# Middle stage: x^T by 256-byte loads and VectorE's 32x32 transposes, q, k and v as three fp32r products, mask in two instructions

## The reference

```python
Q, K, V = (X @ Wq.T, X @ Wk.T, X @ Wv.T)          # 16 heads of 16
KV  = einsum('blhd,blhe->blhde', K, V)
Y   = einsum('blhd,blhde->blhe', Q, cumsum(KV, axis=1))
Bm  = Lm @ swapaxes(Lm, -2, -1)                    # Lm = Ltri * tril
Y   = einsum('hed,blhd->blhe', Bm, Y).reshape(...)
out = Y @ Wc.T
x = x + 0.5 * ffn(layernorm(x)); x = x + attn(layernorm(x)); x = x + 0.5 * ffn(layernorm(x))
```

## Time and profile before

| | us |
|---|---|
| median of three runs (2888.28 to 2891.92) | 2888.59 |
| the profiled execution's own time | 2889.19 |
| its span, first to last instruction | 2887.4 |
| TensorE busy (95%) | 2743.9 |
| TensorE weight loads busy (86%) | 2480.5 |
| VectorE busy (59%) | 1702.5 |
| ScalarE busy (45%) | 1311.9 |
| GpSimd busy (42%) | 1202.6 |

### The profile page before, as it was taken

One profiled execution on the slowest core, in us unless ns is written; L12 is line 12 of the kernel. 1 busy time (PEld: TensorE's weight loads), 2 busy tenths in 40 slices (PEclk: granted clock), 3 DMA queues, 4 the chain that ended last, 5 costly groups with the idle time before them and its releaser, 6 DMA issues.

```text
span 2887.4 us, 56040 instructions
## 1 busy us (share of the span) xinstructions
PE 2743.9 (95%) x18295; PEld 2480.5 (86%) x18295; DVE 1702.5 (59%) x4037; ACT 1311.9 (45%) x2765; POOL 1202.6 (42%) x1550
## 2 busy tenths in 40 slices
PE   4499999999999999989999995999999999999999
PEld 3389899999999989878888884898999998999988
DVE  8754555465555555457878875445555454555554
ACT  5644444454444444334444443444444444444443
POOL 3744444545454545310111122454445454454543
PEclk8699999999999999999999997999999999999999
DMA  8644345353434343221111013434344434434332
GB/s 246 202 99 93 62 92 103 57 100 60 99 61 97 64 92 63 47 62 35 56 62 59 32 46 98 99 58 89 72 97 80 79 60 94 100 58 101 62 53 41
DMA packets 320886, 233.07 MB, mean 81 GB/s; under 512 B 181296, under 2 KB 292784, under 8 KB 320688
## 3 DMA queue, kind: packets, MB, share of 16 engines
q0 software_dynamic: 62688, 87.11, 18.7%
q1 hardware_dynamic: 247712, 133.06, 18.1%
q10 hardware_dynamic: 10288, 10.38, 1.1%
HBM read 124.32 MB, written 78.79 MB: 70 GB/s over the span
## 4 chain that ended last, share of the span: by engine, by line
PE 52%; DVE 3%; issue 1%; ACT 0%; DVEq 0%; POOL 0%; DMA 0%; ACTq 0%; POOLq 0%
PE e_ps L106 8%; PE e_ps L107 8%; PE e_ps L108 8%; PE e_psy L1248 5%; PE mi_qk L1534 3%; PE e_psx L1248 3%; PE e_psy L1250 3%; PE mi_sc L1550 2%; PE mi_yo L1570 2%; PE e_psx L1250 2%; PE mi_yo L1597 2%; PE mi_xv L1540 2%; DVE mi_prob L1715 1%; PE mi_kv L1584 1%; PE mi_yo L1561 1%
## 5 line engine op out<-in xcount | busy, mean ns | idle before, releaser
L1367 DVE TENSOR_TENSOR e_hid<-e_ps,e_gate 128x384 f32<-128x384 f32 (+1 forms) x640 | 382.5, 598 | 394.0 <-ACT e_gate L1306 392.7
L1375 DVE TENSOR_TENSOR e_h_lo<-e_hid,e_h_hi 128x384 fp32r<-128x384 f32 (+1 forms) x640 | 385.0, 602 | 257.3 <-ACT e_h_hi L1310 257.3
L1306 ACT ACTIVATE e_gate<-e_ps 128x384 f32<-128x384 f32 (+1 forms) x640 | 335.4, 524 | 441.1 <-PE e_ps L108 427.7
L1310 ACT ACTIVATE e_h_hi<-e_hid 128x384 fp32r<-128x384 f32 (+1 forms) x640 | 357.2, 558 | 360.8 <-DVE e_hid L1367 348.8
L106 PE MATMUL e_ps<-e_xT_hi,c_wa 128*128 128x384 f32 (+1 forms) x1280 | 448.9, 351 | 5.6 <-issue 5.3
L107 PE MATMUL e_ps<-e_xT_lo,e_wb 128*128 128x384 f32 (+1 forms) x1280 | 450.6, 352 | 0.0
L106 PE MATMUL e_ps<-e_xT_hi,e_wb 128*128 128x384 f32 (+1 forms) x1280 | 450.5, 352 | 0.0
L108 PE MATMUL e_ps<-e_xT_hi,e_wb 128*128 128x384 f32 (+1 forms) x1280 | 450.5, 352 | 0.0
L107 PE MATMUL e_ps<-e_xT_lo,c_wa 128*128 128x384 f32 (+1 forms) x1280 | 448.4, 350 | 0.0
L108 PE MATMUL e_ps<-e_xT_hi,c_wa 128*128 128x384 f32 (+1 forms) x1280 | 448.2, 350 | 0.0
L467 POOL DMA_INDIRECT c_xrow<-normed_rows,e_token x320 | 352.4, 1101 | 153.3 <-POOL e_token L1133 77.9
(11 more groups left out here) (305 smaller groups left out, 4755.3 us busy)
## 6 DMA issues: line engine op xcount, KB each, us to landing
c_raw<-w SPq DMA_DIRECT2D x544, 64.0 KB, 2.6
e_spread<-c_xrow SPq DMA_DIRECT2D x608, 32.0 KB
c_raw<-w SPq DMA_DIRECT2D x68, 256.0 KB, 4.1
e_spread<-c_xrow SPq DMA_DIRECT2D x640, 24.0 KB
normed_rows<-r_xn SPq DMA_DIRECT2D x8, 1056.0 KB, 7.1
normed_rows<-mi_xn SPq DMA_DIRECT2D x8, 1056.0 KB, 4.9
x<-x ACTq DMA_DIRECT2D x8, 1024.0 KB, 12.3
out<-mi_x SPq DMA_DIRECT2D x8, 1024.0 KB, 5.3
```

Source lines behind the costliest of these rows:

```text
L1306: act.activation(gate[:, f % 2, 0:n], ps1[f % 2][:, 0:n], ACT.Silu).then_inc(gated, 1)
L1310: act.activation(h[0][:, f, 0:n], hid[:, f % 2, 0:n], ACT.Copy).then_inc(h_high, 1)
L1367: dve.tensor_tensor(hid[:, f % 2, 0:n], ps3[f % 2][:, 0:n], gate[:, f % 2, 0:n], ALU.mult).then_inc(hid_ready, 1)
L1375: dve.tensor_tensor(h[1][:, f, 0:n], hid[:, f % 2, 0:n], h[0][:, f, 0:n].bitcast(F32), ALU.subtract).then_inc(h_ready, 1)
```

## The change

In the middle stage, chunks go in pairs for x^T, q and k. x^T of a pair no longer comes from TensorE: SyncE loads x1 again from DRAM in blocks of 32 rows by 64 columns (four DMAs a pair, 256 bytes a piece), VectorE transposes their 32x32 squares in one instruction (`square`), ScalarE rounds the result to fp32r (`high_x`), GpSimd subtracts (`low_x`). q and k of the pair and v of each chunk become three fp32r products each. q of a pair is made in the odd steps and k in the even ones, in one bank after the other; ScalarE's copies of q and k have 512 columns in place of 256. k's turn goes to v's bank and waits until v is kept. The mask is two instructions of 1024 columns. The rows of the weights are permuted by the host to fit the order in which squares come out. The steps begin at -6. GpSimd's picked rows are now tied to steps 4 and 5. In the routing stage ScalarE and VectorE split the centred weights into a high and a low part; some of Setup's tiles now lie in the expert stage's row tile, so `keep_heads` also waits for the low part.

```diff
@@ class Setup
+    def split_high(self, act):
+        k = self.k
+        act.wait_ge(self.centered, 1)
+        act.activation(k.wqk[0][:], self.raw_qk[:], ACT.Copy)
+        act.activation(k.wvr[0][:], self.raw_vr, ACT.Copy).then_inc(self.heads_ready, 1)
+
+    def split_low(self, dve):
+        k = self.k
+        dve.wait_ge(self.heads_ready, 1)
+        dve.tensor_tensor(k.wqk[1][:], self.raw_qk[:], k.wqk[0][:].bitcast(F32), ALU.subtract)
+        dve.tensor_tensor(k.wvr[1][:], self.raw_vr, k.wvr[0][:].bitcast(F32), ALU.subtract).then_inc(self.centered, 1)
...
     def keep_heads(self, act):
-        act.wait_ge(self.heads_made, 1)
+        act.wait_ge(self.heads_made, 2)
+        act.wait_ge(self.centered, 2)
...
@@ route_phase, ScalarE: for each group g, behind the normalisation of group g+1
+                    if g == 0:
+                        su.split_high(act)
                     if g == 1:
                         su.keep_heads(act)
@@ route_phase, VectorE: at the end of group g
                     if g == 0:
                         su.center(dve)
+                    if g == 1:
+                        su.split_low(dve)
@@ middle_phase, SyncE
+                for n in STEPS:
+                    if pair_at(n + 6) is not None:
+                        spread_rows(pair_at(n + 6))
+                    if n == -6:
+                        load(1)
+                        load(2)
...
@@ middle_phase, GpSimd
+                def low_x(p):
+                    pool.wait_ge(x_high, p + 1)
+                    pool.tensor_tensor(xT[p % 2][1][:], turned[:], xT[p % 2][0][:].bitcast(F32),
+                                       ALU.subtract).then_inc(x_low, 1)
+
+                for n in STEPS:
+                    g, c = divmod(n, MG)
+                    if pair_at(n + 4) is not None:
+                        low_x(pair_at(n + 4))
+                    if c in (4, 5) and 1 <= g < MGS:
+                        r.pick_rows(pool, g - 1, (g - 1) % 2, MQ * (g - 1) + c - 4, c - 4)
@@ middle_phase, TensorE
+                def project_q(p):
+                    pe.wait_ge(x_low, p + 1)
+                    wait(pe, qk_kept, 2 * p)
+                    for blk in range(KD):
                         for kk in range(KD):
+                            ins = mm3(pe, qk[:, blk * 2 * P:(blk + 1) * 2 * P], wqk(kk, blk),
+                                      (xT[p % 2][0][:, kk, :], xT[p % 2][1][:, kk, :]), kk == 0, kk == KD - 1)
                     ins.then_inc(qk_made, 1)
...
                 def turn_k(n):
-                    pe.wait_ge(q_kept, n + 1)
+                    pe.wait_ge(qk_kept, n // 2 * 2 + 2)
+                    pe.wait_ge(v_kept, n + 1)
...
                 for n in STEPS:
                     g, c = divmod(n, MG)
-                    if chunk(n + 2):
-                        project_qk(n + 2)
+                    if pair_at(n + 3) is not None:
+                        project_q(pair_at(n + 3))
+                    if pair_at(n + 2) is not None:
+                        project_k(pair_at(n + 2))
+                    wait(pe, kr_kept, min(n + 2, NCH))
...
@@ middle_phase, ScalarE, step n
+                    if pair_at(n + 3) is not None:
+                        keep_q(pair_at(n + 3))
+                    if pair_at(n + 2) is not None:
+                        keep_k(pair_at(n + 2))
                     if chunk(n + 2):
...
+                        keep_v(n + 2)
                     if chunk(n):
                         keep_y(n)
                     if chunk(n + 2):
                         keep_krow(n + 2)
-                    if chunk(n + 3):
-                        keep_x(n + 3)
+                    if pair_at(n + 4) is not None:
+                        high_x(pair_at(n + 4))
@@ middle_phase, VectorE
-                    for i in range(4):
-                        dve.tensor_tensor(prob[n % 2][:, i], sc[:, i, :].rearrange("p (h t) -> p h t", h=4),
-                                          k.causal[:].unsqueeze(1).broadcast_to([P, 4, P]),
+                    for i in range(0, 4, 2):
+                        dve.tensor_tensor(prob[n % 2][:, i:i + 2].rearrange("p i h t -> p (i h) t"),
+                                          sc[:, i:i + 2, :].rearrange("p i (h t) -> p (i h) t", h=4),
+                                          k.causal[:].unsqueeze(1).broadcast_to([P, 8, P]),
...
+                    if pair_at(n + 5) is not None and n > -2:
+                        square(pair_at(n + 5))
```

More of the change, by code:

```diff
@@ L1464, in middle_phase, with pair_at, own @@
         xn2_stored = [m.sem(f"xn2_stored{b}") for b in range(2)]
-        vzero = m.sem("vzero")
         tab_kept = m.sem("tab_kept")
         x1_g, x2_g, xn_g = (groups_of(t) for t in (x1_in, x2_out, xn_out))
-        STEPS = range(-2, NCH + TAB + 1)
+        STEPS = range(-6, NCH + TAB + 1)
+        PAIRS = NCH // 2
+        SPREADS = 16 * QUARTERS
+        def pair_at(n):
+            return n // 2 if n % 2 == 0 and chunk(n) else None
+        def own(n):
+            return slice(n % 2 * P, n % 2 * P + P)
         def chunk(n):
@@ L1491, in load, with spread_rows @@
                     sp.dma_start(x1[:, g % 3], x1_g[g]).then_inc(x_loaded[g % 3], 16)
-                load(1)
-                load(2)
-                for g in range(MGS):
-                    sp.wait_ge(x2_ready, MG * (g + 1))
-                    sp.dma_start(x2_g[g], x2[:, g % 2]).then_inc(x2_stored[g % 2], 16)
-                    if g + 3 < MGS:
-                        load(g + 3)
-                    sp.wait_ge(xn2_made, MG * (g + 1))
-                    sp.wait_ge(r.gated, g + 1)
-                    sp.dma_start(xn_g[g], xn2[:, g % 2]).then_inc(xn2_stored[g % 2], 16)
+                def spread_rows(p):
+                    wait(sp, x_squared, p)
+                    for j in range(QUARTERS):
+                        rows = x1_in[p * 2 * P:(p + 1) * 2 * P, j * KD * SQ:(j + 1) * KD * SQ]
+                        sp.dma_start(spread[j * SQ:(j + 1) * SQ, :, :],
+                                     rows.rearrange("(u s) d -> s u d", s=SQ)).then_inc(x_spread, 16)
+                for n in STEPS:
[5 more added lines that the diff above has]
+                    g, c = divmod(n, MG)
+                    if c == 0 and 1 <= g < MGS + 1:
+                        sp.wait_ge(x2_ready, MG * g)
+                        sp.dma_start(x2_g[g - 1], x2[:, (g - 1) % 2]).then_inc(x2_stored[(g - 1) % 2], 16)
+                        if g + 2 < MGS:
+                            load(g + 2)
+                    if c == 4 and 1 <= g < MGS + 1:
+                        sp.wait_ge(xn2_made, MG * g)
+                        sp.wait_ge(r.gated, g)
+                        sp.dma_start(xn_g[g - 1], xn2[:, (g - 1) % 2]).then_inc(xn2_stored[(g - 1) % 2], 16)
                 for b in range(2):
@@ L1520, in _, with wqk @@
             def _(pe):
-                def turn_x(n):
-                    wait_x1(pe, *divmod(n, MG))
-                    wait(pe, v_kept, n)
-                    for half in range(KD):
-                        ins = pe.transpose(xv[:, half * P:(half + 1) * P],
-                                           x1[:, n // MG % 3, n % MG, half * P:(half + 1) * P], k.ident[:])
-                    ins.then_inc(xt_made, 1)
-                def project_qk(n):
-                    pe.wait_ge(xT_ready, n + 1)
-                    wait(pe, kr_kept, n)
-                    for blk in range(2 * KD):
-                        for kk in range(KD):
-                            ins = pe.matmul(qk[:, blk * P:(blk + 1) * P], k.wqk[:, kk, blk * P:(blk + 1) * P],
-                                            xT[n % 2][:, kk, :], start=(kk == 0), stop=(kk == KD - 1))
+                def wqk(kk, blk):
+                    return tuple(part[:, kk, blk * P:(blk + 1) * P] for part in k.wqk)
@@ L1536, in project_qk @@
                     ins.then_inc(qk_made, 1)
                 def project_v(n):
+                    high, low = xT[n // 2 % 2]
                     for kk in range(KD):
-                        ins = pe.matmul(xv[:, 0:WV], xT[n % 2][:, kk, :], k.wvr[:, kk, :],
-                                        start=(kk == 0), stop=(kk == KD - 1))
+                        ins = mm3(pe, xv[:, 0:WV], (high[:, kk, own(n)], low[:, kk, own(n)]), (k.wvr[0][:, kk, :], k.wvr[1][:, kk, :]),
+                                  kk == 0, kk == KD - 1)
@@ L1549, in scores @@
                             rows = slice(32 * i, 32 * i + 32)
-                            ins = pe.matmul(sc[:, i, half * 2 * P:(half + 1) * 2 * P], kT[n % 2][rows, half, :],
-                                            qeo[n % 2][rows, half].rearrange("p a t -> p (a t)"),
+                            ins = pe.matmul(sc[:, i, half * 2 * P:(half + 1) * 2 * P], kT[n // 2 % 2][rows, half, own(n)],
+                                            qeo[n // 2 % 2][rows, n % 2, half].rearrange("p a t -> p (a t)"),
```

(13 more changed lines are left out.)

121 lines of the change are left out of this document (59 added, 62 removed).

## The result

The changed kernel takes 2917.22 us (median of four runs, 2913.34 to 2919.08) by 2890.26 for the kernel before (2888.28 to 2893.54): 1.0094 of it, interval 1.0082 to 1.0106, slower. The forecast was 2911, with a range of 2892 to 2930. The profiled execution took 2913.34 us, its span 2911.4, at a granted clock of 0.975; the sum of the prediction, 2911.6, is made against this kind of number. It is the fastest of the four, though: by medians the change costs 27.0 us, in the two profiled executions 24.0, and the sum said 22.4.

The account below looks back on a forecast made before the run. The prediction took TensorE to bound the middle stage and ScalarE's queue to set the routing stage's end. It summed 2889.2 + 12.2 routing + 10 start + 3.0 six full groups - 2.8 last group = 2911.6, given as 2911, range 2892 to 2930.

Parts of the forecast that it names:

- Routing, +12.2: Routing stage: keep_heads on ScalarE waits for VectorE's split_low, so group 3's normalisation comes later; +12.2 us, between 8 and 13.
- the routing hides its wait: Routing stage: the wait disappears in the slow issue of copies, +1 in place of +12, 2899 us; chance 0.08.
- Start, +10: Start of the middle stage: loads, square, high and low parts precede the first q; chunk 0 10 us later, bounds 6 and 14.
- Hand-over: Middle stage, odd steps: q waits 1.65 us for GpSimd's subtraction; two steps take 14.35 us, where they took 14.36.
- the walk: Middle stage: eight steps timed by TensorE's output and VectorE's addition; 59.6 us with rounding, +0.5 for each of six groups.
- VectorE: Middle stage: mask -0.13 us a step, transposition 0.62 to 0.70 in odd steps; work 53.5 a group, 52.1 before, below 59.
- the ranks' wait: Middle stage, step 3: VectorE reads the ranks 1.0 us later, since ScalarE keeps q of two chunks before v.
- The last chunks, -2.8: Middle stage, last group, which ends without q, k and turn of k: -2.8 us.
- The rival on the other side: Middle stage: the hand-over's 1.65 us is hidden, full groups take 57.0; 2886 us, no change; chance 0.12.
- The clock rival: Middle stage: each 1.65 us idle drops TensorE to half clock, some 1.5 us a pair, +48, 2959 us; chance 0.05.

Follow-up runs that it names:

- low_early: The changed kernel with VectorE making the weights' low part before reading group 1's ranks, in place of after that group's picks: 2910.93 us, 1.0066 of the kernel before.
- low_twice: The changed kernel with GpSimd's subtraction done twice for each pair, the first into a tile nobody reads: 2985.98 us, 1.0328 of the kernel before.
- high_early: The changed kernel with ScalarE's high_x behind the keeping of v, in place of behind the copy of k's rows: 2913.66 us, 1.0085 of the kernel before.
- moments_together: stats_seven with VectorE's moments of x1 for the next group interleaved with x2's in step 0, from the second group on: 2888.85 us, 0.9999 of the kernel before.
- stats_seven: The changed kernel with low part and high_x earlier, squares behind the addition, start loads reordered, x1 statistics in steps 6 and 7: 2888.99 us, 1.0006 of the kernel before.

## Why the prediction was right

The two large terms and both mechanisms behind them were right: ScalarE's wait for the low part in the routing stage, and GpSimd's pass on the path of each pair. That the sum comes within 2 us of the profiled execution is in part luck. The terms missed by -2.1, -0.2, +0.8, +3.1 and -0.3, which cancel in part, and by medians the change costs 27.0 where the sum said 22.4.

- **Routing, +12.2, measured +10.1.** The wait for the low part ended at 76.74 (76.2 forecast). Behind it, the work up to the next normalisation took 9.6 us, not 11.1: the two copies (the forecast once says three) are now issued in 1.37 us in place of 2.22, and ScalarE no longer waits between its own two copies of the head products, 0.4 us. Of the 11.4 by which that normalisation is late, 10.1 reach the end of the expert stage. The bounds (8 to 13) held it. low_early takes 7.8 of it back at that mark by removing this wait alone, so the rival "the routing hides its wait" is out.
- **Start, +10, measured +9.8.** Less the 10.1 us by which the stage is late, q starts at 1269.2 (1268.9 forecast), k at 1274.0 (1273.7), the step of chunk 0 at 1285.3 (1284.9). The half clock of the first products is there. The agreement to 0.4 hides two errors that cancel: the four loads are issued in 1.8 us and not 2.4, and the last lands 4.0 after its issue and not 2.6. By low_early's 39.36 the same code could as well have read +11.8.
- **Hand-over.** The wait and its releaser were right in each odd step; low_twice shows that it is on the path. The term was sized 0.22 too small a pair (14.35 forecast, 14.57 read): q takes 1.52 (1303.09 to 1304.61) and not 1.37, mostly since the product behind the first comes 0.23 later and not 0.12, and v takes 0.74 and not 0.70. Four pairs a group make that 0.9, which is the 0.8 of the first group. In a full group VectorE's waits take part of it: with a wait 0.22 longer, the walk gives 60.0 in place of 59.7. That is 0.3 of the 0.5 by which a full group was missed (1.02 read, 0.5 forecast); the rest stays open.
- **VectorE.** The mask pair took 2.36 (2.27 to the next instruction, as forecast), the transposition 0.70, the ranks' wait was there (5.7 us in six groups, 1.0 each forecast), and the heavy step's 8.31 is the walk's 8.3.
- **The last chunks, -2.8, measured -3.1.** This agreement is the clock's: the kernel before shows 0.96 in that stretch and the changed kernel 1.00. In low_early, with the same code and 0.96, the stretch takes 43.46, which would be -1.4.
- **The rival on the other side was wrongly priced.** A hidden hand-over was to give 2886. high_early hides it and takes 2913.66. The walk let VectorE's lateness cost what it lasts; it missed the half clock behind some idles of about 2 us and VectorE's longer work beside GpSimd's in steps 2 and 5. With VectorE's work spread and the other two terms taken down, the same idea reaches 2889, no change.
- **The clock rival** stood against the idle of 1.65 and had 0.05: right for 1.44, where the full groups show 1.00. But the clock was not to be left aside for the other rivals: in low_twice it goes with 30 of the 69 us, and in high_early, by the estimate above, with some 2.4 of the 4.0 by which a full group exceeds the walk's 57.0. Nor was the row behind it (0.91 for a state product) one of half clock throughout, where high_early's product takes 1.22.

No version ran faster than both kernels by more than can be told. Without the hand-over the new products save TensorE 6 us in eight chunks (a group without heavy steps takes 51.4 in moments_together and 57.4 before), and by that VectorE becomes the bound of the full groups.

## What to carry to other kernels

When an edit takes work from the engine that bounds a step, walk the step again with the next engine in line, and list what stands behind each new wait in every queue: here the hand-over inside each pair cost the whole saving, and a wait in another stage and a later start, neither of which the change's title names, made it a loss. Short idles of TensorE are priced by their length only while the granted clock stays up, so look at the clock of the window before counting on it.

## What the runs showed of the hardware

- A VectorE instruction of 128 x 64 fp32 in SBUF took 1.10 us in place of 0.20 when it started during a GpSimd subtraction of two SBUF inputs, and ended with it (1426.06 and 1426.01). The mask, read from PSUM, was not stretched beside the same pass, nor were the statistics, which read one SBUF tile (0.43 at 1316.91 in the changed kernel, inside the pass that starts at 1316.34). The Trainium skill (GPSIMD Engine Reference, Specifications) says that GpSimd shares its SBUF interfaces with VectorE; the trace agrees. The forecast weighed this rule for GpSimd's pass, which stayed at 1.26 to 1.27 in all 32 pairs of the changed kernel; it was VectorE that paid. In high_early four of the passes beside a stretched instruction took 1.33 to 1.34 themselves. No run tested it apart from these coincidences.
- TensorE's granted clock after idles of one length went either way: 1.22 us for the state product behind an idle of 1.86, 0.71 behind another of 1.86, with the scores behind them in 2.09 and 1.15. Each of the two followed another idle (1.25 and 1.23 us) by 9 us. Behind a third, of 1.87 at 1481.51, the state product took 0.71 and the scores 1.97, so the fall came a little later. The Trainium skill (TensorE: Matmul & The Clock Gate, Part 1) says that the place of the clock's change varies from run to run of one kernel. That the spread of 15 us of stats_seven comes from this is not shown; its fastest execution has a mean clock of 0.975, its two slowest 0.971 and 0.972. What decides it here stays open.
